# Ten gathers of the second pass fetched row by row from ScalarE's queue, with a ring of 15 instead of 17

## The reference

```
# x: (6250, 256); src, dst, edge_type: (206250,); relation: (500, 256)
h     = layernorm(x)
m     = clifford_linear(h[src] * relation[edge_type], msg_w, msg_b)
m     = m * sigmoid(relation[edge_type] @ gate_w.T + gate_b)
m     = m * max(deg[src] * deg[dst], 1) ** -0.5
agg   = segment_sum(m, dst)
x     = x + clifford_linear(h + agg, upd_w, upd_b)
# then: score every node, take the upper half, and give those the output of a
# 256 -> 1024 -> 256 feed-forward part, scaled by the score
```

## Time and profile before

| | |
|---|---|
| median of 3 runs | 3807.58 us (3805.44 to 3810.59) |
| the profiled execution | 3818.35 us, its span 3816.5 us |
| mean granted clock of TensorE | 0.951 |
| busy in the span | PE 88%, DVE 73%, POOL 66%, ACT 25% |
| gathers of the second pass (L870) | 1666, 0.958 us each, from 1614.3 to 3717.5 us |
| chain that ended last | PE 35%, DVE 28%, POOL 21%, issue 10%, DMA 5% |

### The profile page before, as it was taken

One profiled execution on the slowest core, in us unless ns is written; L12 is line 12 of the kernel. 1 busy time (PEld: TensorE's weight loads), 2 busy tenths in 40 slices (PEclk: granted clock), 3 DMA queues, 4 the chain that ended last, 5 costly groups with the idle time before them and its releaser, 6 DMA issues.

```text
span 3816.5 us, 71190 instructions
## 1 busy us (share of the span) xinstructions
PE 3367.9 (88%) x23981; PEld 2710.2 (71%) x23981; DVE 2782.5 (73%) x8724; ACT 944.8 (25%) x2408; POOL 2522.8 (66%) x2524
## 2 busy tenths in 40 slices
PE   6836999999999999688999999999999999999995
PEld 6734777777777777466777777777777777777774
DVE  8988999999999998466666666666666666666654
ACT  4041344434443444201111111111111111111111
POOL 1002777777777777377777777777777777777770
PEclk9756999999999999799999999999999999999997
DMA  5341565565555556375555555555555555555552
GB/s 147 82 165 49 159 164 159 161 162 158 162 162 161 160 160 167 99 228 143 138 138 138 139 141 139 139 135 144 138 138 139 135 144 138 139 139 141 139 125 69
DMA packets 286473, 542.03 MB, mean 142 GB/s; under 512 B 78816, under 2 KB 191728, under 8 KB 286116
## 3 DMA queue, kind: packets, MB, share of 16 engines
q0 software_dynamic: 133728, 387.52, 39.1%
q1 hardware_dynamic: 132852, 132.94, 11.9%
q10 hardware_dynamic: 19536, 17.02, 1.5%
HBM read 492.60 MB, written 44.66 MB: 141 GB/s over the span
## 4 chain that ended last, share of the span: by engine, by line
PE 35%; DVE 28%; POOL 21%; issue 10%; DMA 5%; ACT 2%; DVEq 0%; SPq 0%; POOLq 0%; ACTq 0%
POOL arena L870 21%; PE psE L995 6%; PE psE L1035 4%; DMA arena<-t_d,srci 3%; PE psE L1050 3%; PE psE L1271 3%; DVE relw L1863 3%; PE psT L980 3%; PE psY L980 3%; DVE arena L1750 2%; PE psE L1252 2%; DVE X L1997 2%; DVE arena L1838 2%; DVE X L1999 2%; PE psY L958 2%
## 5 line engine op out<-in xcount | busy, mean ns | idle before, releaser
L870 POOL DMA_INDIRECT arena<-t_d,srci x1666 | 1595.4, 958 | 562.9 <-issue 536.1
L923 POOL DMA_INDIRECT X<-t1b_d,srci x840 | 915.2, 1090 | 632.1 <-DMA t1b_d<-arena 278.3
L995 PE MATMUL psE<-arena 128*128 128x257 f32 x3430 | 1039.5, 384 | 54.3 <-DVE arena L1903 52.5
L1903 DVE TENSOR_TENSOR arena<-arena,psT 128x257 f32<-128x257 f32 x858 | 349.1, 421 | 392.3 <-PE psT L980 220.8
L1903 DVE TENSOR_TENSOR arena<-arena,psY 128x257 f32<-128x257 f32 x857 | 349.0, 421 | 384.9 <-PE psY L980 213.7
L995 PEld LDWEIGHTS psE<-arena 128*128 128x128 f32 x3430 | 530.5, 190 | 112.0 <-DVE arena L1903 41.2
L1035 PE MATMUL psE<-arena,X 128*128 128x256 bf16 (+1 forms) x3675 | 534.9, 276 | 0.0
L980 PE MATMUL psT<-relw,arena 126*128 126x257 bf16 x2799 | 452.9, 274 | 16.0 <-DVE arena L1894 16.0
L980 PE MATMUL psY<-relw,arena 126*128 126x257 bf16 x2793 | 450.0, 273 | 0.0
L1050 PE MATMUL psE<-X 128*128 128x256 bf16 (+1 forms) x2520 | 400.9, 275 | 16.0 <-DVE X L1880 8.1
L1035 PEld LDWEIGHTS psE<-arena,X 128*128 128x128 bf16 x3675 | 349.5, 99 | 54.9
(11 more groups left out here) (355 smaller groups left out, 4383.6 us busy)
## 6 DMA issues: line engine op xcount, KB each, us to landing
arena<-types_d SPq DMA_DIRECT2D x245, 220.5 KB
arena<-t_d,srci POOLq DMA_INDIRECT x1666, 3.2
X<-t1b_d,srci POOLq DMA_INDIRECT x840
arena<-acc_d SPq DMA_DIRECT2D x98, 130.0 KB
t1b_d<-arena SPq DMA_DIRECT2D x7, 1347.5 KB, 6.6
arena<-dst_p SPq DMA_DIRECT2D x400, 1.5 KB
arena<-src_p SPq DMA_DIRECT2D x400, 1.5 KB
acc_d<-arena ACTq DMA_DIRECT2D x1, 6370.0 KB, 22.5
```

The source lines that it names most:

```text
L870: pool.indirect_dma_start(gath[:, n % RG, :], None, t2_d, bass.IndirectOffsetOnAxis(ap=srci[:, n:n + 1], axis=0)).then_inc(s_g[n % RG], 16)
L923: pool.indirect_dma_start(ring1[:, n % RG1, :], None, t1b_d, bass.IndirectOffsetOnAxis(ap=srci[:, at:at + 1], axis=0)).then_inc(s_g[n % RG ...
L995: ins = nc.tensor.matmul(psE[:, b % 2, 0:DW], sel[:, n // SG % 3, k % SG, :], rows_of(n), start=False, stop=(k == C - 1))
L1903: v.tensor_tensor(rows, rows, psR[n % BANKS][:, 0:DW], ALU.mult).then_inc(s_po, 1)
```

## The change

Ten slots leave GpSimd's list: slot 17 of blocks 8, 12, 16, ... and 44. Their 128 rows are fetched by 128 plain transfers each, one row of 260 floats to one partition, issued from ScalarE's queue, 8 of them ahead of each of its steps 4 to 19 of a turn of 20 steps (four blocks), during the four blocks before the one that uses the slot. The rows go to one of two buffers, `lone`, outside the ring. SP first writes the ten columns of indices to a small HBM tensor `lone_d` in the order of rows, ScalarE loads one list of 128 to a single partition (step 1 of the turn), and reads 8 indices at a time into registers. The ring `gath` has 15 places instead of 17, and a gather n waits for `summed(n - 14)`. Nothing is changed in the first pass or after the second.

```
--- before.py
+++ after.py
@@ -31,7 +31,7 @@
 NP = 125
 PER = E // NP
 GROUPS = PER // GRAN
-RG = 17
+RG = 15
 
 
 
@@ -95,6 +95,8 @@
 TRIALS = 7
 COUNTS = DIGITS + 3
 EPS = 1e-5
+LONE = 10
+LONE_AT = 17
 UT = E // NP
 SK = 1
 U = 7
@@ -169,6 +171,7 @@
         x1_d = nc.dram_tensor("x1_d", (NB * P, D), F32).ap()
         src_p = nc.dram_tensor("src_p", (E + ROOMY,), I32).ap()
         dst_p = nc.dram_tensor("dst_p", (E + ROOMY,), I32).ap()
+        lone_d = nc.dram_tensor("lone_d", (LONE, P), I32).ap()
         types_d = nc.dram_tensor("types_d", (RANKS * RB * C, P), F16).ap()
         relw_d = nc.dram_tensor("relw_d", (R, DW), F32).ap()
         acc_d = nc.dram_tensor("acc_d", (NB * P, W), F32).ap()
@@ -372,6 +375,10 @@
         o = RG * W + SG * P + ROOM * P
         own_rows = work[:, o:o + 2 * W].rearrange("p (r w) -> p r w", w=W)
         o += 2 * W
+        lone = work[:, o:o + 2 * W].rearrange("p (r w) -> p r w", w=W)
+        o += 2 * W
+        lone_src = work[0:1, o:o + P].bitcast(I32)
+        o += P
         f1 = work[:, o:o + 2 * H].rearrange("p (t n) -> p t n", t=2)
         o += 2 * H
         f2 = work[:, o:o + HT * D].rearrange("p (t n) -> p t n", t=HT)
@@ -579,6 +586,7 @@
         s_umm = [sem(f"s_umm{layer}") for layer in range(2)]
         s_uadd = [sem(f"s_uadd{layer}") for layer in range(2)]
         s_turn = sem("s_turn")
+        s_lone = [sem(f"s_lone{k}") for k in range(2)]
         s_tb = [sem(f"s_tb{h}") for h in range(2)]
         s_g = [sem(f"s_g{k}") for k in range(RG)]
         s_uload = [[sem(f"s_uload{layer}{k}") for k in range(SK)] for layer in range(2)]
@@ -591,15 +599,29 @@
         def loads(n):
 
             k = n % RG
-            return len([m for m in range(k, n + 1, RG) if m % C]) + (len(range(k, C * FETCHED, RG1)) if k < RG1 else 0)
+            mine = len([m for m in range(k, n + 1, RG) if m % C and lone_at(m) < 0])
+            return mine + (len(range(k, C * FETCHED, RG1)) if k < RG1 else 0)
+
+        def lone_slot(i):
+
+            return C * (4 * i + 8) + LONE_AT
+
+        def lone_at(n):
+
+            i = (n // C - 8) // 4
+            return i if 0 <= i < LONE and n == lone_slot(i) else -1
 
         def rows_of(n):
 
+            if lone_at(n) >= 0:
+                return lone[:, lone_at(n) % 2, 0:DW]
             return gath[:, n % RG, 0:DW] if n % C else own_rows[:, n // C % 2, 0:DW]
 
         def landed(n):
 
             h, i = n // C % 2, n // C // 2
+            if lone_at(n) >= 0:
+                return s_lone[lone_at(n) % 2], 16 * P * (lone_at(n) // 2 + 1)
             if n % C:
                 return s_g[n % RG], 16 * loads(n)
             return s_wl[h], 16 * (2 * WINS * len(range(h, COUNTED, 2)) + i + 1)
@@ -826,6 +848,9 @@
             load_types(0)
             load_types(1)
             load_own(1)
+            sp.dma_start(lone_d.rearrange("i p -> p i"),
+                         srci[:, C * 8:C * 8 + LONE * 4 * C].rearrange("p (i k) -> p i k", k=4 * C)[:, :, LONE_AT],
+                         allow_slow_non_contiguous=True).then_inc(s_src, 16)
             for n in range(2, NB * SPB):
                 if n % SPB == SPB - 1 and n // SPB + 1 < NB:
                     load_old1(n // SPB + 1)
@@ -863,7 +888,7 @@
 
             def gathers():
                 for n in range(SLOTS):
-                    if n % C == 0:
+                    if n % C == 0 or lone_at(n) >= 0:
                         continue
                     if n >= RG:
                         pool.wait_ge(s_mm, summed(n - RG + 1))
@@ -1619,7 +1644,30 @@
                                   x1_d.rearrange("(b p) d -> p b d", p=P)[:, 7 * c:7 * c + 7, :]).then_inc(s_xl, 16)
                 act.dma_start(f1, w1.rearrange("(t p) n -> p t n", p=P)).then_inc(s_w, 16)
                 act.dma_start(f2, w2.rearrange("(t p) n -> p t n", p=P)).then_inc(s_w, 16)
+                def lone_sources(i):
+
+                    if i == 0:
+                        act.wait_ge(s_src, 32)
+                    act.dma_start(lone_src, lone_d[i:i + 1, :]).then_inc(s_src, 16)
+
+                def lone_rows(i, j):
+
+                    if j == 0:
+                        act.wait_ge(s_src, 16 * (i + 3))
+                        if i >= 2:
+                            act.wait_ge(s_mm, summed(lone_slot(i - 2) + 1))
+                    act.load(firsts, lone_src[0:1, NODES * j:NODES * j + NODES])
+                    for k in range(NODES):
+                        first = act.snap(firsts[k], min_val=0, max_val=N - 1)
+                        e = NODES * j + k
+                        act.dma_start(lone[e:e + 1, i % 2, :], t2_d[bass.ds(first, 1), :]).then_inc(s_lone[i % 2], 16)
+
                 for n in range(SPB, LAST + 26):
+                    i, j = n // (4 * SPB) - 1, n % (4 * SPB)
+                    if 0 <= i < LONE and j == 1:
+                        lone_sources(i)
+                    if 0 <= i < LONE and j >= 4:
+                        lone_rows(i, j - 4)
                     for m in due2(n, 24):
                         fed_rows(2 * m)
                     for m in due2(n, 25):
@@ -1643,6 +1691,7 @@
                     for m in due(n, 5):
                         sums_out(m)
 
+            firsts = [act.alloc_register(f"lone_first{k}") for k in range(NODES)]
             first_pass()
             act.wait_ge(s_sq, 4)
             nc.scalar.activation(inq[:, :], inq[:, :], ACT.Sqrt).then_inc(s_sqd, 1)
```

More of the change, by code:

```diff
@@ L1621, in second_pass, with lone_sources, lone_rows @@
                 act.dma_start(f2, w2.rearrange("(t p) n -> p t n", p=P)).then_inc(s_w, 16)
-                for n in range(SPB, LAST + 26):
+                def lone_sources(i):
+                    if i == 0:
+                        act.wait_ge(s_src, 32)
+                    act.dma_start(lone_src, lone_d[i:i + 1, :]).then_inc(s_src, 16)
+                def lone_rows(i, j):
+                    if j == 0:
+                        act.wait_ge(s_src, 16 * (i + 3))
+                        if i >= 2:
+                            act.wait_ge(s_mm, summed(lone_slot(i - 2) + 1))
+                    act.load(firsts, lone_src[0:1, NODES * j:NODES * j + NODES])
+                    for k in range(NODES):
+                        first = act.snap(firsts[k], min_val=0, max_val=N - 1)
+                        e = NODES * j + k
+                        act.dma_start(lone[e:e + 1, i % 2, :], t2_d[bass.ds(first, 1), :]).then_inc(s_lone[i % 2], 16)
+                for n in range(SPB, LAST + 26):
+                    i, j = n // (4 * SPB) - 1, n % (4 * SPB)
+                    if 0 <= i < LONE and j == 1:
+                        lone_sources(i)
+                    if 0 <= i < LONE and j >= 4:
+                        lone_rows(i, j - 4)
                     for m in due2(n, 24):
```

## The result

| | before | after |
|---|---|---|
| median | 3805.44 us (5 runs, 3802.29 to 3810.59) | 3824.37 us (5 runs, 3823.45 to 3832.93) |
| ratio, 95% interval | | 1.0052, 1.004 to 1.0064 |
| profiled execution | 3818.35 us | 3829.24 us |
| first gather to last | 2103.2 us | 2119.8 us |

The change makes the kernel slower by 18.9 us by the medians. The forecast was +10.6 us and 3818.2 us. Direction and the range of 3808 to 3832 were right; the narrower range that its own bounds gave, 3812 to 3824, was missed by 0.4 us; the loss was under-estimated by nearly half.

The account below looks back on a forecast made before the run. GpSimd's gather chain was taken to bound the kernel. Ring +20.9, ten gathers -12.6 and 2.3 eaten gave +10.6 us on 3807.58, so 3818.2 us; range 3808 to 3832, by its own bounds 3812 to 3824.

Parts of the forecast that it names:

- What bounds: Second pass: GpSimd's gathers, one every 1.263 us, set the end; TensorE, busy 1872 of 2000 us, does not.
- The ring: GpSimd's gathers: 15 places instead of 17 add 22.1 us of waits in 16 clusters, 20.9 new; bounds 17 to 25.
- The rule: A gather that must wait for a ring place starts 0.27 us after the group of slots it needs is summed.
- Ten gathers: GpSimd's queue: ten gathers fewer at 1.263 us each take 12.6 us off.
- 2.3 us eaten: Part of the 12.6 us gain lost because skipped gathers fill the ring earlier before TensorE's bursts; bounds 0 to 12.6.
- a block of the list: Block with a predicted ring wait; each skipped slot's next block was said to have one in slots 4 to 14.
- SP's list: Start of the pass: writing 1280 indices ahead of the third group's types costs 0, up to 4.4 us.
- rival D: SP's list delays the start by its upper bound and the first cluster grows: 3820 us; counted within the forecast's 0.70.
- ScalarE: Fetching the rows takes ScalarE 6.2 us of an 8.8 us step and costs 0; bound 8 us in all.
- Rival B: ScalarE late from about 0.75 us a row (7.7 us a step), its copies holding up TensorE: 3838 us; chance 0.12.
- The profile's own level: Profiled execution forecast at 3829.0 us, from 3818.35 before plus 10.6; unprofiled median taken as 10.8 us lower.

Follow-up runs that it names:

- the kernel with two queues: Against the kernel before: ring kept at 17, twenty slots leave GpSimd, ten by ScalarE's queue and ten by SP's; 3781.38 us, ratio 0.9943.
- the kernel with twenty slots on one queue: Against the kernel before: ring kept at 17, twenty slots leave GpSimd, all fetched by ScalarE's queue, 16 rows a step; 3819.99 us, ratio 1.0041.
- the late list: Changed kernel, ring 15, with SP's index list written after the thirteenth group of types instead of before the third; 3819.57 us, ratio 1.0039 against before.

## Why the prediction was right in direction and too small

- **What bounds.** Right, with one exception. The end moved with GpSimd's chain of gathers, and TensorE's 94% busy time was no bound: the kernel with two queues takes 22.6 us off with TensorE doing the same work. The exception is the kernel with twenty slots on one queue, where a late ScalarE holds TensorE, and TensorE the places.
- **The ring.** Right in mechanism and in the sum. 22.1 us of waits were expected, 20.9 of them new; ring 15 alone has 25.5 in its trace and 19.7 in its time. The rule was read off one wait in one trace and gives the total for 16, 15 and 14 places, but not each single wait.
- **Ten gathers.** 12.6 us by count, 10.3 after the fuller rings. With 17 places the measured gain is 10.6. With 15 it is 19.7 - 13.8 = 5.9 us by the medians, the late list included. With five runs of each kernel and the intervals given, that difference is uncertain by some 7 us either way, and the traces do not bear a smaller gain out: apart from the list's own waits (9.5 and 2.3 us) the changed kernel has 27.4 us of waits and the one with the late list 20.9, against 25.5 with the ring of 15 alone. Whether 2.3 us eaten was too little is therefore not shown. One reading behind it was wrong: not every skipped slot is followed by a block of the list; the successors of 16, 28 and 40 are not on it.
- **The step that failed: SP's list.** It was put at 0, "up to 4.4 us if that store is used up", and rival D had it at 3820 (the forecast and 4.4 us make 3822.6). It costs 11.2 us with 17 places, and the changed kernel's trace shows a wait of 9.5 us for it. So D named the mechanism, at half its size or less. Two things were wrong. The 4.4 us went by the queue's mean packet time, 0.055 us. The list's packets were shorter than that, and the time was lost by the transfers beside and behind them, which the estimate did not have. And the two groups "in store" were taken for cover, but at the start nothing had been built up: the types that went out at 1624 had been used at once at 1632 in the kernel before, and now landed at 1642.
- **ScalarE.** The cost of 0 was right, at 4.0 us a step instead of 6.2. The 2.0 us that the prediction quoted from the Trainium skill ("DMA: Bandwidth & Descriptors", Anatomy of one DMA) are given there for transfers that GpSimd issues. On ScalarE's queue a row took 3.25 / 8 = 0.41 us, and 1280 of these transfers cost 0.3 us in all. Rival B was refused for ten slots and came true for twenty: there a step has 8.25 us of issuing ahead of the copy, above the 7.7 us a step that the prediction named, though a row took 0.47 us and not the 0.75 it had in mind.
- **The profile's own level.** 3829.0 us was forecast for the profiled execution and 3829.24 came. That is luck: the reference trace was 9 us long and the list's miss about as large.

By the medians the change is ring +19.7, ten gathers beside that ring -5.9, list early rather than late +5. These add up to 19 by construction, each being the step from one kernel to the next, and the last two could shift several us from one to the other. By the changed kernel's own trace the account is: 36.9 us of waits, of which 9.5 are the list's and 27.4 the ring's, against 24.4 forecast. Of the 12.5 us more, the list is three quarters. This trace is 4.9 us above the kernel's median, which is the larger part of why it shows more than the 8.3 us that the median missed by. Why 1280 single elements slow the other transfers is open: nothing here separates their number from their size of 4 bytes or from HBM as their target. The runs show where it costs and not the mechanism.

## What to carry to other kernels

Where one engine's issue chain sets the end, price a smaller buffer by the releases: for each issue, take the end of the group that it would then need, and sum the excess over clusters. It told 16, 15 and 14 places apart from one trace, in the sum and not wait by wait. Look for the buffer's memory and semaphores in what a later stage has not begun to use, before taking it from a ring that is nearly full. A one-off transfer of single elements belongs where nothing behind it is due soon; here it went out at 1616.8 us and types that followed it landed at 1642. Moved issuing work goes to each idle queue in portions that leave room: 4.0 us in a step of 8.8 cost nothing here, 8.25 us did, and between these nothing was tried.

## What was not expected of the hardware

- A transfer of 1280 single 4-byte elements from SBUF to HBM held up transfers of other queues too: 219 instead of 340 GB/s over 17 us, while the DMA engines' busy share was 1.00 against 1.07, and VectorE waited 9.8 and 11.4 us for types issued behind it. Ring 15 alone, without the list, has 340 GB/s in the same window. The Trainium skill has two sentences on this ("DMA: Bandwidth & Descriptors", Rules for kernel authors and Specifications): a non-contiguous last dimension becomes one descriptor per element, and a transfer below 512 bytes is done as a read-modify-write. The first agrees with the 1121 additional packets under 512 bytes in that stretch. On the second no run here tells anything.
- A load of 8 registers takes 0.72 us on ScalarE's queue, where SP's load of 16 took 3.46 us. Half of the latter, 1.73 us, was the estimate. In the kernel with two queues SP's own loads of 8 take 0.78 us, so the queue is not what differs; what does, beside the number, is open. The same page of the Trainium skill (Latency and other measured facts) gives a floor of about 0.6 us for such a load, and the 0.72 us are near it; the 3.46 us for 16 are not.
- A row transfer of 1 KB at an address from a register takes ScalarE's queue 0.234 us, less than half of the 0.62 us of its 64-row transfers, and 0.41 us with the work on the address.
